# Adding the exponentials of two steps elementwise so that one round of the small constant serves both

## What is computed

```python
scores = jnp.einsum('bhtd,bhsd->bhts', q, k) / SCALE
scores = jnp.where(causal[None, None], scores, NEG_INF)
attn = jax.nn.softmax(scores, axis=-1)
mask = jnp.clip((R + z[:, :, None, None] - dist) / R, 0.0, 1.0)
attn = attn * mask
attn = attn / (attn.sum(axis=-1, keepdims=True) + 1e-08)
out = jnp.einsum('bhts,bhsd->bhtd', attn, v)
```

## Time and profile before

| | |
|---|---|
| median of 3 runs | 3382.35 us (3378.8 to 3837.4) |
| profiled execution | 3385.04 us, span 3383.3 us |
| PE busy | 3034.2 us, 90% of the span |
| DVE busy | 1907.4 us, 56% |
| ACT busy | 1067.1 us, 32% |
| POOL busy | 962.4 us, 28% |

### The profile page before, as it was taken

How to read it: one execution, slowest core, us unless ns; L and a number is a source line. 1 busy time by engine, 2 the same in 40 slices (tenths; PEclk the granted TensorE clock), 3 DMA queues, 4 the chain that set the end, 5 groups by cost and what they waited for, 6 DMA issues and landing times. The chain is left out here.

```text
span 3383.3 us, 56216 instructions
## 1 busy us (share of the span) xinstructions
PE 3034.2 (90%) x19448; PEld 1704.5 (50%) x19448; DVE 1907.4 (56%) x2294; ACT 1067.1 (32%) x2526; POOL 962.4 (28%) x628
## 2 busy tenths in 40 slices
PE   7997799999999999999999669999999777777788
PEld 6886333333333333333333558888888342332345
DVE  4333778788787878787887435555554510000038
ACT  3222244444444444444444223333333101110113
POOL 0000544544444454444444112222222000000013
PEclk9998699999999999999999779999999888887879
DMA  4455413121221212131212411122111669999944
GB/s 150 149 198 189 95 51 74 45 70 51 57 64 51 73 42 61 52 75 46 66 51 57 140 53 63 62 68 71 62 62 62 230 246 420 420 421 420 420 170 163
DMA packets 189156, 450.10 MB, mean 133 GB/s; under 512 B 18206, under 2 KB 54744, under 8 KB 164393
## 3 DMA queue, kind: packets, MB, share of 16 engines
q1 hardware_dynamic: 181929, 436.73, 37.3%
q10 hardware_dynamic: 7040, 10.77, 0.9%
HBM read 363.28 MB, written 83.89 MB: 132 GB/s over the span
## 5 line engine op out<-in xcount | busy, mean ns | idle before, releaser
L681 ACT ACTIVATE B_e<-B_pS 128x512 f32<-128x512 f32 (+3 forms) x1288 | 621.7, 533 | 894.5 <-PE B_pS L775 459.0
L537 POOL TENSOR_TENSOR B_em<-B_e,B_mask 128x1024 f32<-128x1024 f32 (+1 forms) x322 | 675.5, 2099 | 758.5 <-ACT B_e L681 716.5
L594 DVE TENSOR_REDUCE B_mx<-B_pM 128x4 f32<-128x2048 f32 (+1 forms) x320 | 627.3, 1960 | 43.7 <-PE B_pM L734 22.5
L772 PE MATMUL B_pS<-B_qs,B_ks 128*128 128x512 f32 (+3 forms) x1288 | 505.9, 446 | 26.4 <-issue 23.2
L587 DVE SCALAR_TENSOR_TENSOR B_em<-B_mask,B_e 128x1024 f32<-128x1024 f32 (+1 forms) x322 | 352.7, 1096 | 218.8 <-PE B_pN L802 217.1
L772 PEld LDWEIGHTS B_pS<-B_qs,B_ks 128*128 128x128 f32 x1288 | 229.2, 192 | 342.0 <-issue 226.9
L790 PE MATMUL B_pD<-B_e,B_tiny 128*32 128x512 f32 (+3 forms) x2560 | 309.6, 556 | 0.0
L796 PE MATMUL B_pD<-B_em,B_ones 128*32 128x512 f32 (+3 forms) x2560 | 300.1, 541 | 0.0
L802 PE MATMUL B_pN<-B_em,B_v 128*32 128x512 f32 (+3 forms) x2560 | 293.6, 531 | 0.0
L1987 PE MATMUL E_pI<-ring,hT 128*32 128x512 f32 x1024 | 185.3, 817 | 101.1 <-DMA ring<-in_L_ffn_e_W_dram 58.0
L1910 DVE TENSOR_TENSOR E_ug<-E_pT,bT 128x32 f32 x32 | 5.7, 192 | 445.7 <-PE E_pT L1997 445.7
(11 more groups left out here) (286 smaller groups left out, 4846.8 us busy)
## 6 DMA issues: line engine op xcount, KB each, us to landing
ring<-in_L_ffn_e_W_dram SPq DMA_DIRECT2D x128, 1024.0 KB, 21.8
ring<-in_L_ffn_e_Wg_dram SPq DMA_DIRECT2D x64, 1024.0 KB, 23.6
B_qs<-q_hi SPq DMA_DIRECT2D x72, 256.0 KB, 4.6
B_ks<-k_hi SPq DMA_DIRECT2D x72, 256.0 KB, 3.9
A_xin<-in_x_dram SPq DMA_DIRECT2D x10, 1024.0 KB, 13.3
B_kh<-k_hi SPq DMA_DIRECT2D x36, 256.0 KB, 2.7
B_qh<-q_hi SPq DMA_DIRECT2D x36, 256.0 KB, 3.7
B_qs<-q_lo SPq DMA_DIRECT2D x36, 256.0 KB, 4.0
```

The lines of the kernel that those rows point to most:

```text
L537: nc.gpsimd.tensor_tensor(em[:, f % SLOTS_EM, DVE_HEADS:, w0:], e[:, f % SLOTS_E, DVE_HEADS:, w0:], mask[:, DVE_HEADS:, u0:u0 + BLK - w0], ...
L594: nc.vector.tensor_reduce(mx[:, :, qt, c], pM[:, :, 0:w], AX.X, ALU.max).then_inc(max_taken, 1)
L681: nc.scalar.activation(e[:, f % SLOTS_E, h, w0:], pS[:, h % SBANKS, w0:], ACT.Exp, scale=SCALE).then_inc(exp_ready, 1)
L772: last = nc.tensor.matmul(pS[:, h % SBANKS, w0:], ks[:, kb // NT, h, kb % NT * P:(kb % NT + 1) * P], qs[:, qb, h, w0:], start=True, stop=( ...
```

## The change

In a pair of full steps (f - 1 even, f odd) the two exponential tiles are added elementwise, in place, into the slot of f - 1: POOL adds heads 0 and 1 ahead of its `weigh(f)` and head 2 behind it, DVE adds head 3 at the start of its turn f + 1. PE's `mix(f - 1)` issues no product with `tiny`, and `mix(f)` waits for both adds and makes one round of `tiny` from the summed slot. POOL's first add also waits until DVE has weighed f - 1, since it overwrites what that reads. The ring `em` grows from 2 to 4 slots, so that neither half of `weigh(f)` waits for `mix(f - 2)`, but for `mix(f - 4)`. ACT's wait for a free slot of `e` is one step longer where the slot held a pair's sum. Diagonal steps are as before.

```diff
-SLOTS_E, SLOTS_EM = 4, 2
+SLOTS_E, SLOTS_EM = 4, 4
...
+PAIRS = sum(qb * NT // 2 for qb in range(BPB))
...
+def full(f):
+
+    qb, kb = FLAT[f % STEPS]
+    return kb < NT * qb
+
+
+def pair_opens(f):
+
+    return full(f) and f % 2 == 0
+
+
+def pair_closes(f):
+    return full(f) and f % 2 == 1
...
+            def add(it, f, heads):
+
+                pool.wait_ge(exp_ready, it * HPG * STEPS + HPG * f + heads[-1] + 1 + SBANKS)
+                if heads[0] < DVE_HEADS:
+                    pool.wait_ge(masked, it * STEPS + f)
+                else:
+                    pool.wait_ge(masked_last, it * STEPS + f)
+                at = slice(heads[0], heads[-1] + 1)
+                return nc.gpsimd.tensor_tensor(e[:, (f - 1) % SLOTS_E, at, :], e[:, (f - 1) % SLOTS_E, at, :],
+                                               e[:, f % SLOTS_E, at, :], ALU.add)
...
                 for f in range(2, STEPS + 2):
+                    if pair_closes(f):
+                        add(it, f, (0, 1))
                     weigh(it, f)
+                    if pair_closes(f):
+                        add(it, f, (2,)).then_inc(added_by_pool, 1)
...
+            def add(it, f):
+
+                dve.wait_ge(exp_ready, it * HPG * STEPS + HPG * (f + 1) + SBANKS)
+                dve.wait_ge(masked_last, it * STEPS + f)
+                nc.vector.tensor_tensor(e[:, (f - 1) % SLOTS_E, HPG - 1, :], e[:, (f - 1) % SLOTS_E, HPG - 1, :],
+                                        e[:, f % SLOTS_E, HPG - 1, :], ALU.add).then_inc(added_by_dve, 1)
...
+                    if pair_closes(f - 1):
+                        add(it, f - 1)
...
-                        act.wait_ge(mixed, it * STEPS + STEPS + f + 1 - SLOTS_E)
+                        act.wait_ge(mixed, it * STEPS + STEPS + f + 1 - SLOTS_E + pair_opens(f - SLOTS_E))
...
-                pe.wait_ge(exp_ready, it * HPG * STEPS + HPG * (f + 1) + SBANKS)
-                for h in range(HPG):
-                    cols = slice(h * DH, (h + 1) * DH)
-                    nc.tensor.matmul(pD[cols, w0:], tiny[:, :], e[:, f % SLOTS_E, h, w0:],
-                                     start=first, stop=False, tile_position=(0, h * DH))
+                if not pair_opens(f):
+                    slot = f % SLOTS_E
+                    if pair_closes(f):
+                        pe.wait_ge(added_by_pool, pairs_until(it, f))
+                        pe.wait_ge(added_by_dve, pairs_until(it, f))
+                        slot = (f - 1) % SLOTS_E
+                    else:
+                        pe.wait_ge(exp_ready, it * HPG * STEPS + HPG * (f + 1) + SBANKS)
+                    for h in range(HPG):
+                        cols = slice(h * DH, (h + 1) * DH)
+                        nc.tensor.matmul(pD[cols, w0:], tiny[:, :], e[:, slot, h, w0:],
+                                         start=first, stop=False, tile_position=(0, h * DH))
...
-                                     start=False, stop=final, tile_position=(0, h * DH))
+                                     start=first and pair_opens(f), stop=final, tile_position=(0, h * DH))
```

More of the change, by code:

```diff
@@ L353, in offset, with pairs_until @@
     return qb * BLK - kb * P + width(f)
+def full(f):
[5 more added lines that the diff above has]
+    return full(f) and f % 2 == 1
+def pairs_until(it, f):
+    return it * PAIRS + sum(pair_closes(g) for g in range(f % STEPS + 1)) + f // STEPS * PAIRS
 def block_end(f):
@@ L418, in self_attention @@
         mixed = sem("B_mixed")
+        added_by_pool = sem("B_added_by_pool")
+        added_by_dve = sem("B_added_by_dve")
         den_out = sem("B_den_out")
```

## The result

The changed kernel takes 3627.95 us (median of 4 runs, 3622.97 to 3631.73) against 3381.39 us before: ratio 1.0735, 95% interval 1.0721 to 1.075. It is slower by some 247 us. The median before is of four runs, of which one took 3837.4 us in a slow execution; the ratio goes by the fast runs alone.

A forecast was written before the change was run, and what follows sets the result against it. PE was taken to bound the kernel before, and what POOL and DVE hold in turn after. Twelve pairs' extras gave 17.7 us an iteration, +142 us over eight, so 3524 us; range 3435 to 3640.

The forecast's parts named there:

- The direction and the mechanism: Full steps: slower, 4.2% more, because POOL and DVE don't run weighings and adds side by side; slower had 84%.
- the sum: Loop: extra time of 12 pairs, 17.7 us an iteration, over 8 iterations +142 us.
- PE's side: Full steps on PE: one `tiny` round of 0.88 us less in each of 96 pairs, 84 us.
- The prices of the adds: POOL and DVE: adds cost what same-size products do: 2.33 to 2.38 us two heads, 1.29 one head, DVE 0.69.
- The exclusion: DVE and POOL in full steps: each holds something the other needs, POOL 2.2 us for two heads, DVE 1.1 a weighing.
- The larger ring as free: Ring `em`: removes DVE's 211.2 us of waits for `mix`, which were slack, so it gives no time.
- the rival that PE stays the bound: Full steps: POOL's adds fit beside DVE's work, the 84 us come through, 3298 us; chance 5%.
- the time of a pair: Pair of full steps: DVE's and POOL's held times together 10.7 us against 9.62, POOL hardly ever idle.
- The 2.0 taken off: First full step of two blocks: PE already waits 0.98 us for DVE, POOL's added time lies beside it; -2.0 us an iteration.
- The third rival: Full steps: late reductions delay scores, exponentials and POOL, +1.5 us a pair, PE's clock may fall; 3667 us, chance 17%.
- the sign that the prediction gave for being wrong in this way: Profile after, full steps: POOL shows idle time though PE waits, which would point to a chain through all three engines.
- The marks named: Profile after: POOL above 80% busy, its 1024-column instructions about 2.9 us, DVE's weighing over 1.26, PE waits, pairs every 10.7 us.

The follow-up runs named there:

- the kernel without adds: The changed kernel without either engine's add, one `tiny` round for each pair from the even step's slot alone: 3302.22 us, ratio 0.976.
- The fills: The changed kernel with POOL's two adds replaced by fills of an unused tile that read nothing, DVE's add and all waits kept: 3478.06 us, ratio 1.0284.
- the late kernel: The changed kernel with a pair's `tiny` round moved behind the rounds of em with ones and v in the odd step: 3572.94 us, ratio 1.055.

## Why the prediction was right, and where its size was off

**The direction and the mechanism held.** The measured 3628 us lie in the range, near its upper end; the sum gave +142 us where +247 were measured.

**PE's side.** "96 x 0.88 = 84 us": the kernel without adds is 80 us faster than before. Right.

**The prices of the adds.** Taken from products of the same size. DVE's add took 0.68 us unheld against 0.69 assumed, POOL's two-head add 2.35 to 2.36 us against 2.33 to 2.38. Right.

**The exclusion.** The hand-overs of 2.2 and 1.1 us were read from rows 8 and 9, and POOL's 1.1 for one head worked out from them; they come back in the changed kernel within 0.03 us. The fills show that a busy POOL alone does not exclude: nearly as long busy, but reading nothing, it gives 150 us back.

**The larger ring as free, and the rival that PE stays the bound.** The ring changed nothing (0.9999). The rival had 5% and needed the adds to fit beside DVE's work; they don't.

**The term that was mis-sized** is the time of a pair, "together **10.7 us**, with POOL hardly ever idle". The hold times in it are right, but POOL does not stand full, and so the pairs are longer than what they hold. The steps 13 to 16 shown above do not yet show it: with a pair's two reciprocals (0.9) and a final product (1.1) in them the sum has 2 x 10.7 + 2.0 = 23.4 us, and they took 23.65. That agreement is luck, since POOL idles 2.62 us in them, which the sum does not have. The whole of one iteration, the fourth, shows it, four steps at a time, each from the end of one `mix` to the end of the one four steps later. First before, then after, for steps 24 to 27:

```profile
1053.51:1074.05 20.54, 19.30 (x146) 7.08 (x146) 15.13 (x14) 9.67 (x18) 11.42 (x6) 1.00 0.17 39
```

```profile
1160.82:1187.84 27.02, 21.76 (x130) 7.12 (x130) 26.23 (x17) 9.66 (x18) 24.91 (x11) 0.81 0.16 40
```

| steps | before, us | after, us | grown by | in the sum | granted clock after |
|---|---|---|---|---|---|
| 4 to 7 | 20.58 | 24.32 | 3.7 | 1.4 | 0.93 |
| 12 to 15 | 19.42 | 23.81 | 4.4 | 3.1 | 0.86 |
| 16 to 19 | 19.43 | 24.18 | 4.8 | 3.3 | 0.86 |
| 24 to 27 | 20.54 | 27.02 | 6.5 | 1.4 | 0.81 |
| 28 to 31 | 19.26 | 25.00 | 5.7 | 4.3 | 0.93 |
| 32 to 35 | 19.48 | 25.80 | 6.3 | 4.2 | 0.88 |
| together | 118.71 | 150.13 | 31.4 | 17.7 | |

(The 2.0 taken off stands here half at steps 4 to 7, half at 24 to 27; the clock before is 1.00 in all six.) So a pair took 12.5 us on the mean, and the growth is 13.7 us more than in the sum, 110 us for eight iterations; the sum was short by 105. The sum fell short most where the clock is lowest. POOL is busy 126.4 of the 150.1 us, so it idles 24 us an iteration where the sum had it full.

The unevenness was not foreseen: of the twelve pairs of that iteration four took 8.9 to 9.1 us, close to PE's own 8.74, and the others 11.3 to 16.8. I had spread the wait evenly, 2 us in each pair, and on that ground left the clock out: "With shorter waits between full work no row shows it, so I leave it out of the sum". In fact the waits bunch to 3.31 us and the like, the size of that at the turn of an iteration, and behind them the clock falls as it did there. The same PE work is busy 124 us longer in the changed kernel than without the adds. How much of that lies on the path is not settled. Keeping PE at work ahead of the adds gave 33 us net while adding 169 us of work, and shifting the wait by two rounds gave 55 us together with PE's shorter wait; but in the late kernel more work raised the clock and cost 46 us.

**The third rival** (the chain and the clock, 17%, 3667 us) was thus partly true. Its sign in the profile is there: POOL waits 145.1 us for exponentials ahead of its two-head weighings, and it is busy 1208.17 of 1735 us, 70%, where I had named above 80%. So is the sign that the prediction gave for being wrong in this way: POOL idle in full steps though PE waits. The forecast and this rival should not have been priced apart, since one brings about the other, and the measured time lies between the two.

**The marks named.** DVE's weighing over 1.26: 2.34. POOL's near 2.9: 2.77 and 2.53. `tiny` rounds "1.0 us long still": wrong behind the long waits, 1.93 us. Waits ahead of `tiny` that POOL's one-head add ends: 2.2 us on the mean, up to 3.8. Waits ahead of `unit` for DVE's reduction: 130.9 us, more than for the adds. "A pair of full steps every 10.7 us": 12.5.

## What to carry to other kernels

VectorE's weighings, adds and mask pieces and GpSimd's products and adds, all on tiles in SBUF, ran here as one resource; VectorE's reductions and reciprocals did not share in it. Add up what each holds, from rows where they met, and compare the sum with the step, before moving work there from a busy TensorE. That sum is only a lower bound; the engines' own chains (the run with all adds on VectorE) and the clock behind bunched waits come on top. Where the aim is a cheaper small term of a sum, first look whether it needs its precision: the same round in bf16 from the upper half-words gave about 150 us and added nothing to the other engines. It drops the lower 16 bits of the exponentials, but only in the sum that is multiplied by 1e-8.

## What was not expected of the hardware

- A GpSimd fill that reads nothing doesn't hold VectorE's two-input instruction at all (1.21 us beside it, 46 times), while a GpSimd product of 2.4 us does to its end (up to 3.4 us).
- More TensorE work made the kernel faster, twice: 96 rounds more, 30 us less; 192 rounds more, 33 us less, with the mean granted clock in the loop at 0.93 and 0.96 instead of 0.89. A third time, where TensorE's wait for the adds was already short, 192 rounds more cost 46 us, though the clock rose there too, from 0.92 to 0.95.
- A float32 tile in SBUF can be read as bf16 with a step of two elements by TensorE: four products of 512 columns side by side take 0.24 us, against 0.88 for the same four in float32. No run here has the same round from a packed bf16 tile beside it.
